# Making a scan's first step size at the end of the block before it

## What is computed

```
xz = einsum('bhwc,oc->bhwo', x, in_proj_w);  xi, z = split(xz)
xi = silu(conv2d(xi, conv_w, conv_b))                     # depthwise 3x3: this is u
x_dbl = einsum('bkdl,kcd->bkcl', xs, x_proj_w)            # the "projections"
dts, Bs, Cs = split(x_dbl, [DT_RANK, DT_RANK + D_STATE])  # 6, 16, 16 rows
dts = einsum('bkrl,kdr->bkdl', dts, dt_w)
delta = softplus(dts + dt_bias)                           # the step size
# per step:
dA = exp(delta * A);  h = dA * h + (delta * u) * B;  y = einsum('bkdn,bkn->bkd', h, C)
```

## Time and profile before

| | us |
|---|---|
| median of 3 timed runs (lowest, highest) | 13456.75 (13454.54, 13469.53) |
| the profiled execution's own time | 13459.71 |
| its span, first to last instruction | 13457.9 |
| PE, DVE, ACT, POOL busy | 10568.0, 11944.1, 6832.9, 10383.8 |
| granted TensorE clock, mean | 0.901 |

### The profile page before, as it was taken

One profiled execution on the slowest core, in us unless ns is written; L12 is line 12 of the kernel. 1 busy time (PEld: TensorE's weight loads), 2 busy tenths in 40 slices (PEclk: granted clock), 3 DMA queues, 4 the chain that ended last, 5 costly groups with the idle time before them and its releaser, 6 DMA issues. The chain is left out here.

```text
span 13457.9 us, 95099 instructions
## 1 busy us (share of the span) xinstructions
PE 10568.0 (79%) x24646; PEld 4131.8 (31%) x24646; DVE 11944.1 (89%) x8647; ACT 6832.9 (51%) x10172; POOL 10383.8 (77%) x4597
## 2 busy tenths in 40 slices
PE   6877877778777787777878778777787777877778
PEld 2333323333233332333323333233332333323333
DVE  7999779997799968999679996799968999679996
ACT  4545454554545545555455555555555545555455
POOL 4999459994599945999459994599946999369993
PEclk8899989999899998999989999899998999989999
DMA  4676446774467644677446774477735777357773
GB/s 140 216 219 215 114 131 215 218 214 112 136 214 220 214 107 140 214 219 216 102 143 216 220 214 99 145 216 220 214 96 152 214 220 213 95 151 214 220 214 94
DMA packets 734799, 2404.31 MB, mean 179 GB/s; under 512 B 173200, under 2 KB 175248, under 8 KB 722768
## 3 DMA queue, kind: packets, MB, share of 16 engines
q1 hardware_dynamic: 734192, 2397.58, 61.2%
HBM read 2300.18 MB, written 67.11 MB: 176 GB/s over the span
## 5 line engine op out<-in xcount | busy, mean ns | idle before, releaser
L1262 POOL TENSOR_TENSOR state<-state,c_sb 128x1024 f32<-128x1024 f32 x3072 | 7184.0, 2359 | 463.4 <-ACT carry L1089 461.7
L1018 PE MATMUL ps<-state,wt 128*128 128x512 f32 x12288 | 6328.2, 657 | 165.2 <-ACT ya L1082 107.8
L1018 PEld LDWEIGHTS ps<-state,wt 128*128 128x128 f32 x12288 | 2553.2, 211 | 3051.2 <-issue 2474.3
L1221 DVE TENSOR_TENSOR_SCAN state<-decay,carry,ps 128x1024 f32<-128x1024 f32 x1440 | 3379.2, 2347 | 104.2 <-DVE ps L1208 36.6
L1089 ACT COPY carry<-state 128x1 f32<-128x1 f32 x3072 | 585.3, 191 | 4860.5 <-DVE state L1221 4851.6
L995 PE MATMUL ps<-parts,sel 114*128 114x512 bf16 (+1 forms) x3840 | 1286.3, 420 | 2103.2 <-DVE state L1221 2101.9
L1251 POOL TENSOR_TENSOR dbu<-b_sb,du 128x1024 f32<-128x1024 f32 x1152 | 2719.1, 2360 | 231.0 <-DVE du L1236 231.0
L1208 DVE TENSOR_TENSOR ps<-ps,du 128x1024 f32<-128x1024 f32 x1920 | 2322.2, 1209 | 1.7 <-PE ps L995 0.8
L1131 ACT ACTIVATE decay<-delta,a_neg 128x1024 f32<-128x1024 f32 x1920 | 2194.8, 1144 | 6.9
L1221 DVE TENSOR_TENSOR_SCAN state<-ps,carry,dbu 128x1024 f32<-128x1024 f32 x864 | 2013.1, 2330 | 3.8 <-POOL dbu L1251 2.5
L995 PEld LDWEIGHTS ps<-parts,sel 114*128 114x128 bf16 (+1 forms) x3840 | 260.9, 100 | 3653.2 <-DVE state L1221 3385.8
(11 more groups left out here) (217 smaller groups left out, 10216.9 us busy)
## 6 DMA issues: line engine op xcount, KB each, us to landing
c_sb<-bc SPq DMA_DIRECT2D x2048, 512.0 KB, 4.4
c_sb<-bc SPq DMA_DIRECT2D x2048, 256.0 KB, 5.5
b_sb<-bc SPq DMA_DIRECT2D x768, 512.0 KB, 4.7
b_sb<-bc SPq DMA_DIRECT2D x768, 256.0 KB, 5.4
x_nat<-x SPq DMA_DIRECT2D x17, 1536.0 KB, 14.3
gates<-gate_a SPq DMA_DIRECT2D x8, 2048.0 KB, 6.8
x_tok<-x SPq DMA_DIRECT2D x288, 48.0 KB, 1.8
gn<-gn_t SPq DMA_DIRECT2D x8, 1536.0 KB, 7.1
```

The lines of the kernel that those rows point to most:

```text
L1018: mm = pe.matmul(py[:, q * CH:(q + 1) * CH], col("ident"), state[:, slot(g, n), q * CH:(q + 1) * CH], start=(n == 0), stop=False)
L1221: dve.tensor_tensor_scan(state[:, slot(g, n), way], rate, what, 0.0 if fresh else carry[:, n:n + 1], ALU.mult, ALU.add)\
L1262: pool.tensor_tensor(state[:, slot(g, n), :], state[:, slot(g, n), :], c_sb[:, n % CRING, :], ALU.mult).then_inc(S["weighted"], 1)
```

## The change

The step size of chunk 0 is made in prep_b. Its six matmuls stand between projections 13 and 14 and write ps0, which the convolution has left; they wait for the twelve copies into parts and for the last quarter of u. ACT does Abs, Relu and Exp behind the casts of projection 14, "+ 1" behind those of 15, and Ln and the copy to delta at the end. DVE does its four steps at the end, du included. The buffers delta, du, relu_v and zexp lie where `xf_nat` lies, so ACT and DVE wait until the stores from it have landed; for that the four stores of the row order got a semaphore of their own, `rows_stored`, and the counts of `bc_stored` are four lower. The load of the table with Exp and Ln stands ahead of the first cast. In the scan's block the first softplus and its table load are gone; the loop over chunks is the same.

```diff
@@ -62,6 +62,7 @@
+DT_FROM = 14
@@ -680,7 +681,7 @@
-                            to_rows(sp, 0, 0, g, kind).then_inc(S["bc_stored"], 16)
+                            to_rows(sp, 0, 0, g, kind).then_inc(S["rows_stored"], 16)
@@ -694,7 +695,8 @@
                     sp.wait_ge(S["gates_stored"], 48)
-                    sp.wait_ge(S["bc_stored"], 8 * 16)
+                    sp.wait_ge(S["rows_stored"], 4 * 16)
+                    sp.wait_ge(S["bc_stored"], 4 * 16)
                     sp.wait_ge(S["parts_in"], 12 * 16)
@@ -766,9 +768,21 @@
+                    def first_dt():
+
+                        pe.wait_ge(S["parts_in"], 12 * 16)
+                        pe.wait_ge(S["u_ready"], NCH // SLOTS)
+                        for q in range(2):
+                            for p in range(3):
+                                mm = pe.matmul(ps2[0][:, q * CH:(q + 1) * CH], dt_w[6 * NS:XR3, p, 0, :],
+                                               parts[6 * NS:XR3, 0, q * CH:(q + 1) * CH], start=(p == 0), stop=(p == 2))
+                        mm.then_inc(S["pre_mm"], 1)
+
                     for i in range(2 * SLOTS, 2 * NCH):
                         project_a(i)
                         project_r(i)
+                        if i == DT_FROM - 1:
+                            first_dt()
@@ -809,6 +823,7 @@
                     u_out(3)
+                    ln_exp_tables(act)
@@ -824,11 +839,36 @@
+                    def first_exp():
+                        bias = col("dt_b", 128, 0)
+                        act.wait_ge(S["rows_stored"], 4 * 16)
+                        act.wait_ge(S["pre_mm"], 1)
+                        act.activation(zexp[:, :], ps2[0][:, :], ACT.Abs, bias=bias).then_inc(S["dt_abs"], 1)
+                        act.activation(relu_v[:, :], ps2[0][:, :], ACT.Relu, bias=bias).then_inc(S["dt_relu"], 1)
+                        act.wait_ge(S["dt_abs"], 1)
+                        act.activation(zexp[:, :], zexp[:, :], ACT.Exp, scale=-1.0).then_inc(S["dt_exp"], 1)
+
+                    def first_one():
...
+                        act.activation(ps2[0][:, :], zexp[:, :], ACT.Identity, bias=col("one")).then_inc(S["dt_one"], 1)
+
+                    def first_ln():
+                        act.wait_ge(S["dt_low"], 1)
+                        act.activation(zexp[:, :], zexp[:, :], ACT.Ln, bias=col("one")).then_inc(S["dt_ln"], 1)
+                        act.wait_ge(S["du_ready"], 1)
+                        act.copy(delta[:, :], ps2[0][:, :]).then_inc(S["delta_ready"], 1)
+
                     for i in range(2 * NCH + 1):
                         if i < 2 * NCH:
                             take(i)
                         if i > 0:
                             middle(i - 1)
+                        if i == DT_FROM:
+                            first_exp()
+                        if i == DT_FROM + 1:
+                            first_one()
+                    first_ln()
@@ -892,6 +932,18 @@
+                    dve.wait_ge(S["dt_one"], 1)
+                    dve.scalar_tensor_tensor(ps2[0][:, :], ps2[0][:, :], 1.0, zexp[:, :], ALU.subtract, ALU.subtract)\
+                       .then_inc(S["dt_low"], 1)
...
+                    dve.wait_ge(S["rows_stored"], 4 * 16)
+                    dve.wait_ge(S["delta_sum"], 1)
+                    dve.tensor_tensor(du[:, :], ps2[0][:, :], ua[:, 0:SC], ALU.mult).then_inc(S["du_ready"], 1)
@@ -1056,14 +1108,12 @@
-                    pre_dt(0, 0)
                     each_chunk(steps)
@@ -1063,7 +1113,6 @@
-                    ln_exp_tables(act)
@@ -1149,13 +1199,6 @@
-                    softplus_abs(0, 0)
-                    softplus_relu(0, 0)
-                    softplus_exp(0)
-                    softplus_one(0)
-                    softplus_ln(0)
-                    act.wait_ge(S["du_ready"], 1)
-                    act.copy(delta[:, :], pc[:, :]).then_inc(S["delta_ready"], 1)
                     each_chunk(steps)
@@ -1229,11 +1272,6 @@
-                    softplus_low(0)
-                    softplus_high(0)
-                    softplus_sum(0)
-                    dve.wait_ge(S["delta_sum"], 1)
-                    dve.tensor_tensor(du[:, :], pc[:, :], u_of(0, 0), ALU.mult).then_inc(S["du_ready"], 1)
                     each_chunk(steps)
```

More of the change, by code:

```diff
@@ L275, in build @@
         gn_stored gates_ready gates_stored conv_mm conv_taps u_ready conv_r conv_p conv_sum ur_ready
-        ur_in xp_mm xp_hi xp_out xp_rest xp_mid xp_low parts_zero bc_stored parts_in pre_mm dt_abs
+        ur_in xp_mm xp_hi xp_out xp_rest xp_mid xp_low parts_zero rows_stored bc_stored parts_in pre_mm dt_abs
         dt_relu dt_exp dt_one dt_ln dt_low dt_high delta_sum delta_ready du_ready b_mm decayed dbu_ready
@@ L825, in middle @@
                         act.copy(mid[o][:, sl(j)], rest[:, i % SLOTS, :]).then_inc(S["xp_mid"], 1)
+                    def first_exp():
[7 more added lines that the diff above has]
+                    def first_one():
+                        act.wait_ge(S["dt_exp"], 1)
+                        act.wait_ge(S["dt_relu"], 1)
+                        act.activation(ps2[0][:, :], zexp[:, :], ACT.Identity, bias=col("one")).then_inc(S["dt_one"], 1)
[4 more added lines that the diff above has]
+                        act.copy(delta[:, :], ps2[0][:, :]).then_inc(S["delta_ready"], 1)
                     for i in range(2 * NCH + 1):
@@ L893, in _ @@
                             lowest(i - 1)
+                    dve.wait_ge(S["dt_one"], 1)
+                    dve.scalar_tensor_tensor(ps2[0][:, :], ps2[0][:, :], 1.0, zexp[:, :], ALU.subtract, ALU.subtract)\
+                       .then_inc(S["dt_low"], 1)
+                    dve.wait_ge(S["dt_low"], 1)
+                    dve.tensor_tensor(ps2[0][:, :], relu_v[:, :], ps2[0][:, :], ALU.subtract).then_inc(S["dt_high"], 1)
+                    dve.wait_ge(S["dt_high"], 1)
+                    dve.wait_ge(S["dt_ln"], 1)
+                    dve.tensor_tensor(ps2[0][:, :], zexp[:, :], ps2[0][:, :], ALU.add).then_inc(S["delta_sum"], 1)
+                    dve.wait_ge(S["rows_stored"], 4 * 16)
+                    dve.wait_ge(S["delta_sum"], 1)
+                    dve.tensor_tensor(du[:, :], ps2[0][:, :], ua[:, 0:SC], ALU.mult).then_inc(S["du_ready"], 1)
         def scan():
@@ L954, in steps @@
                         if T == 0 and following[0] == 1:
-                            sp.wait_ge(S["bc_stored"], 12 * 16)
+                            sp.wait_ge(S["bc_stored"], 8 * 16)
                         for n in range(NS):
@@ L1073, in take_y @@
                             act.wait_ge(S["parts_in"], 24 * 16)
-                            act.wait_ge(S["bc_stored"], 12 * 16)
+                            act.wait_ge(S["bc_stored"], 8 * 16)
                         act.wait_ge(S["y_summed"], g + 1)
```

## The result

| | us |
|---|---|
| the kernel before, median of 8 runs | 13456.62 (13450.94 to 13469.53) |
| the changed kernel, median of 8 runs | 13503.83 (13486.93 to 13513.03) |
| ratio, 95% interval | 1.0035 (1.0025 to 1.0045) |
| profiled execution, its span | 13511.1 |

The account below looks back on a forecast made before the run. DVE, busy 89% of the span, was taken as the bound. Per image the 2.2 us gain is lost and 1.8 more: +14.6 us over eight images on 13459.7, 13474.3, less 3.0 for timed runs: 13471, range 13436 to 13490.

Parts of the forecast that it names:

- the likeliest case: First chunk: late loads hold POOL, +0.7 to +2.9 us per image, 13462 to 13480; chance 0.48.
- the opening's loss: From the first scan to that of n = 7: late loads give back the 2.2 us gain and 1.8 more per image.
- the seam's gain: From the projections' end to the first scan: first scan starts 2.2 us earlier per image.
- Part 1: Exp and Ln table load, 1.28 us, moved before ACT's first cast of the projections: costs nothing on ACT.
- Part 2: Six matmuls between projections 13 and 14 take 1.3 us, without waiting for the copies into parts; bounds 0 and 1.3.
- Parts 3 to 5: Projections' end to first scan: block ends at 1879.66 instead of 1869.70, first scan at 1882.3 instead of 1884.52.
- Part 5: Scan's opening without the softplus: gain 2.2 us per image, most of the moved chain not hidden at either place.
- Part 6: SP's loads start 9.9 us later; C for n = 2 lands late, scan of n = 7 starts 1.8 us later.
- rival C: First chunk: loads of C for n = 4 and B for n = 7 late too, +31 us, 13488; chance 0.14.
- rival B: Scan's opening: loads are there in time, the whole 2.2 us remain, -17.8 us, 13439; chance 0.26.
- Rival D: Projections: TensorE waits 1.3 us for parts, block and loads later, +25 us, 13482; chance 0.12, shared with another rival.

Follow-up runs that it names:

- e4: Changed kernel with the six matmuls behind the last projection and all of the softplus behind the last casts: 13496.83 us, ratio 1.0026.
- e5: Changed kernel with e1 and e4 together, and C for n = 0 issued ahead of the first late stores: 13449.46 us, ratio 0.9995.
- e6: Changed kernel with e2 and e4 together: 13451.02 us, ratio 0.9995.
- e1: Changed kernel with SP's first loads, except C for n = 0, issued at the end of the projections' block: 13457.65 us, ratio 1.0001.
- e2: Changed kernel with the sixteen late stores and copies issued at n = 8 to 15 instead of 0 to 7: 13465.72 us, ratio 1.0008.
- e3: Kernel before, with SP's first loads of the scan made to wait until delta is ready: 13526.24 us, ratio 1.0051.
- e8: Kernel before, with SP's first loads issued at the end of the projections' block: 13455.26 us, ratio 1.0000.
- e7: Kernel before, with the late stores and copies at n = 8 to 15: 13451.78 us, ratio 0.9998.

## Why the prediction was wrong

The forecast was 13471, with a range to 13490; 13504 was measured. The mechanism of the likeliest case was right, the sign too. Two terms of its sum were mis-sized: the opening's loss was put at 4.0 us per image and was 6.6, and the seam's gain was put at 2.2 and was 1.0. A third, 1.2 us behind the opening, was not in the sum.

**Part 1**, the table load: nothing in the traces speaks against its being free: ACT still waits 5.58 us for TensorE behind it, in the second image (7.32 in the earlier trace rows). It was not tried alone.

**Part 2**, the six matmuls: they took 1.46 at the new place, from the first's start to the last's end, and projection 14 followed 1.4 behind their start (1.3 was taken). They started at 1865.40 - 4.15 = 1861.25, as forecast. "I take no wait" was right for the second and fourth image and wrong for the other six, where the copies into parts were 0.2 to 0.4 us later than projection 13.

**Parts 3 to 5**, the seam: the working follows the second image well. The block's end was put 9.96 us later; by the timelines it is 1883.98 - 4.15 (the delay brought from the first image, 1864.43 against 1860.28 at projection 13) - 1869.70 = 10.1. The gain was put at 2.2; it was 1.9 in that image and 1.0 in the mean of eight. The step that failed is reading one image for all. Over eight images 7 us are missing against the second: 1.6 by the waits of part 2, and about 5 by TensorE at the lower granted clock, 0.8 us each time, at projection 9 in five images and at projection 15 in one (see e4). Part 5 says that the chain is "not hidden at the new place either". e4 shows it stronger: the new place was worse than no overlap, by 0.6 us and the waits.

**Part 6**, the loads. This is the step that failed, and by its size, not its kind. The landing of C for n = 2 was put at 15.1 us behind SP's start (B for n = 5 stood ahead of it too, besides the loads that the working names); in the second image it is 1890.3 + 9.1 - 1884.33 = 15.1. Over the eight images it is 15.0 to 17.1, 16.0 in the mean, where I had allowed 0.4 either way: 0.9 us too little. POOL waited for it 3.3 to 4.9 us in each image. And I let POOL run from there to n = 7 "all without a gap". The load of C for n = 4 landed 12.3 us after its issue, and POOL waited 1.29 more; over the eight images 1.0 to 2.1, 1.6 in the mean, for a term that the sum had at nothing. The two together make up nearly all of the 2.6 us by which the opening was longer than forecast (6.6 for 4.0). The idle time of DVE before the scans of n = 5 and n = 7 was 5.1 us in the second image and at least 6.1 in the mean, for "about 4". I had this case as rival C, with its place (n = 4) and its point ("more than 11 us"), and held it for less likely than rival B, by which the loads would be in time. Even C's 13488 was too low, and its other half did not come: B for n = 7 landed 20.3 us behind SP's start, 5.4 ahead of POOL's turn in the second image, and C for n = 3 was 2.2 ahead. What the working left out is a count for C for n = 4. Before, SP stood waiting for a free buffer ahead of it, issued it 19.4 us behind its own start, and it took 5.5. Now SP was still issuing what stood ahead when the buffer came free; it issued it 11.0 behind its start, and it took 12.3. The landing at 23.3 was 1.2 us behind the end of POOL's product for n = 3.

**Rival B** fell: the loads were not in time. Where they were (e5, e6), the opening was as before, but its 13439 was not reached, since the seam gave less than 2.2. The formula in the Trainium skill ("DMA: Bandwidth & Descriptors", section "Anatomy of one DMA — SWDGE (gpsimd) path"), an estimate of 3.2 us for 512 KB, is stated for one DMA of GpSimd's path and has no queue in it; the rows of SP's loads have 9.1 and 12.3. The measurement decides.

**Rival D** took part as a term: the wait for parts cost 0.2 to 0.4 us in six images, not 1.3.

**Not foreseen:** "next", +9.6 us over the eight images. Most of it is in the first eight states of the second chunk. They last 27.4 to 27.7 us in five images of the changed kernel and in one of the kernel before, and 25.4 to 26.1 in the other ten. The busy times of these eight states in the first image, changed kernel, then before:

```profile
260.69:288.34 27.65, 24.80 (x52) 8.51 (x51) 25.42 (x14) 14.84 (x22) 26.83 (x12) 0.81 0.70 226
```

```profile
258.75:284.14 25.39, 22.55 (x50) 7.76 (x49) 25.21 (x15) 14.75 (x22) 25.39 (x12) 0.87 0.68 225
```

TensorE had the lower granted clock there, 0.81 against 0.87, and it is 0.81 in all six such stretches. DVE waited 0.54 us for PE in this one, and behind that 1.49 for ACT's carry. Which image it strikes differs from execution to execution: e1, e2, e3 and e4 have it once each, e5 to e8 never. Why the clock falls there was not tested; it stays open whether the change makes it more frequent.

The sum, per image: -1.0 at the seam, +6.6 in the opening, +1.2 in the next stretch, 6.8 in all, times 8 = 54; with -1 elsewhere that is the 53 us by which the profiled executions differ. The forecast had -2.2, +4.0 and nothing.

## What to carry to other kernels

A serial chain that everybody waits for may be the cover of something else. Before moving it, list what each queue, DMA queues above all, does during it, and count the time of those things from their new start to their new need. Count in the issuing engine's own time for every transfer ahead (here SP needed 6 us before the load that came late), and when one load comes out late, work out the landing of each load behind it before calling the rest free. Do it for the image or loop turn with the latest landing too, not for one alone. And a piece that is put "beside" other work is hidden only if the engines it uses had idle time there: here ACT had as much to do either way, and TensorE, which set the pace, got six matmuls more ahead of the last projections.

## What the runs showed of the hardware

A 512 KB load with broadcast to 128 partitions took 3.8 to 4.3 us to landing as the first of the queue (kernel before and changed kernel, eight images each). As the fifth load, behind four stores and two small copies, it took 8.3 to 9.6 before and 9.0 to 10.8 in the changed kernel, and C for n = 5 of the changed kernel 13.4 to 16.0, with more issued ahead of it. In e2, without the stores and copies, the fifth load took 8.7 to 10.2: from issue to landing it was hardly faster, 9.2 in the mean against 9.9.

What the small transfers cost this load was mostly SP's time to issue them. SP issued ten transfers in 5.97 us ahead of it in the changed kernel, and four loads in 1.81 us in e2. With the same start of SP, moving the sixteen late stores and copies away took the opening's loss from 52.9 to 2.7 us.

Single executions of one kernel differ by 20 to 36 us here (13486.93 to 13513.03 for the changed one, 13476.72 to 13512.93 for e4). Each kernel has one trace; between kernels whose edit changed nothing at the marks (e7 and e8 against the kernel before) the traces differ in the stretches which the edits do not touch, by 3.5 and 12.6 us.
